# The order of the small loads on GpSimd's DMA queue at the start of a linear-attention and mixture-of-experts layer

## The reference

```
xn   = layernorm(x)
q,k,v= split(xn @ w_qkv.T + b_qkv)           # 16 heads of 64
q    = silu(q);  k = softmax(k over tokens)
kv   = k^T v per head;  o = q @ kv per head
o    = layernorm(o) * ln_g + ln_b
gate = sigmoid((xn @ w_g1.T + b_g1) @ w_g2.T + b_g2)
attn = (o * gate) @ w_out.T + b_out
logits = xn @ Wr.T; the two best of 8 experts, softmax over the two
ffn  = sum over the two of w * (xn @ We[e]), tokens past a capacity of 769 dropped
out  = x + attn + ffn
```

## Time and profile before

| | us |
|---|---|
| median of 3 runs | 1163.08 (1161.27 to 1163.39) |
| the profiled execution's own time | 1163.06 |
| its span, slowest core (core 0) | 1161.3 |
| spans of the 8 cores | 1150.5 to 1161.3 |
| TensorE busy | 873.4 (75%) |
| DVE busy | 452.8 (39%) |
| ACT busy | 103.6 (9%) |
| POOL busy | 57.8 (5%) |

### The profile page before, as it was taken

The page is one execution under the profiler, slowest core; times in us unless marked ns, Lnnn a source line. Parts: engine busy times, 40 slices in busy tenths (PEclk is TensorE's granted clock), DMA queues, the critical chain, the costliest instruction groups (busy, mean ns, idle before and its releaser), DMA issues.

```text
span 1161.3 us, 11087 instructions; the slowest of 8 cores (1150.5 to 1161.3 us)
## 1 busy us (share of the span) xinstructions
PE 873.4 (75%) x3848; PEld 356.4 (31%) x3914; DVE 452.8 (39%) x692; ACT 103.6 (9%) x123; POOL 57.8 (5%) x58
## 2 busy tenths in 40 slices
PE   0133063499997999650555999999999999999993
PEld 0010021133335433110101334444444444444441
DVE  0123867400332001737685334444444444444441
ACT  0121100122000221141221000000000000000000
POOL 2100000000000000000000000000000000000244
PEclk9975577699998899575555999999999999999997
DMA  2466600000404002200000004040404132231276
GB/s 48 109 169 151 114 1 18 19 1 1 73 1 73 1 1 34 39 0 0 1 1 0 1 1 73 1 73 1 73 6 68 22 53 36 38 50 24 66 242 236
DMA packets 23300, 55.59 MB, mean 48 GB/s; under 512 B 4752, under 2 KB 4752, under 8 KB 22224
## 3 DMA queue, kind: packets, MB, share of 16 engines
q0 software_dynamic: 16160, 29.68, 16.6%
q1 hardware_dynamic: 4208, 12.63, 3.8%
q10 hardware_dynamic: 2880, 12.58, 2.9%
HBM read 76.18 MB, written 8.39 MB: 73 GB/s over the span
## 4 chain that ended last, share of the span: by engine, by line
PE 62%; DVE 17%; DMA 13%; issue 4%; ACT 2%; DVEq 1%; POOL 0%; POOLq 0%; ACTq 0%
PE PS L167 62%; DMA ar<-x_fm 6%; DMA y<-fpool 5%; DVE scr_b L177 5%; DVE ar L177 5%; DVE srow L177 3%; DVE reps L177 1%; ACT bpool L184 1%; DVE qrow L177 1%; DMA wg_sb<-wg_t 1%; ACT qrow L184 1%; DVEq L176 1%; DVE drow L177 0%; DVE crow L177 0%; DMA wr_hi<-wr_t 0%
## 5 line engine op out<-in xcount | busy, mean ns | idle before, releaser
L167 PE MATMUL PS<-ar 128*128 128x512 bf16 (+1 forms) x3135 | 698.2, 377 | 21.2 <-DVE ar L177 9.8
L167 PEld LDWEIGHTS PS<-ar 128*128 128x128 bf16 x3200 | 301.9, 99 | 382.6 <-issue 52.9
L177 DVE SCALAR_TENSOR_TENSOR ar<-PS,lc,ar 128x512 bf16<-128x512 f32 x256 | 192.2, 751 | 251.1 <-PE PS L167 251.1
L177 DVE CAST ar<-PS 128x512 bf16<-128x512 f32 x96 | 66.4, 692 | 167.7 <-PE PS L167 164.5
L167 PE MATMUL PS<-ar,ones_c_b 128*1 128x512 bf16 x64 | 22.5, 487 | 93.4 <-ACT bpool L184 93.1
L177 DVE TENSOR_TENSOR ar<-fpool,ar 128x2048 bf16<-128x2048 f32 x8 | 18.3, 2293 | 90.7 <-DMA ar<-x_fm 90.7
L184 ACT ACTIVATE ar<-PS 128x512 bf16<-128x512 f32 x64 | 38.2, 597 | 93.8 <-PE PS L167 93.7
L198 POOL DMA_DIRECT2D ar<-we x8 | 7.0, 873 | 665.8 <-PE PS L167 665.8
L167 PE MATMUL PS<-bpool,wg_sb 64*128 64x512 bf16 x32 | 18.7, 584 | 28.4 <-DVE ar L177 28.4
L167 PEld LDWEIGHTS PS<-ar,ones_c_b 128*1 128x1 bf16 x64 | 5.2, 92 | 109.2 <-issue 106.8
L191 POOL TENSOR_TENSOR fpool<-ar,fpool 128x1024 f32<-128x1024 bf16 x16 | 34.2, 2137 | 89.9 <-DVE ar L177 62.3
(11 more groups left out here) (109 smaller groups left out, 267.2 us busy)
## 6 DMA issues: line engine op xcount, KB each, us to landing
ar<-we POOLq DMA_DIRECT2D x8, 2048.0 KB, 16.9
fpool<-x_tm SPq DMA_DIRECT2D x16, 512.0 KB, 4.2
y<-fpool ACTq DMA_DIRECT2D x16, 512.0 KB, 4.1
fpool<-x_fm SPq DMA_DIRECT2D x4, 1024.0 KB, 10.0
ar<-x_fm POOLq DMA_DIRECT2D x8, 512.0 KB, 7.2
fpool<-x_fm ACTq DMA_DIRECT2D x4, 1024.0 KB, 7.0
ar<-wk_t POOLq DMA_DIRECT2D x1, 2048.0 KB, 16.7
ar<-wv_t POOLq DMA_DIRECT2D x1, 2048.0 KB, 14.9
```

The lines of the kernel that those rows point to most:

```text
L167: i = eng.matmul(out, l, r, start=start, stop=stop)
L177: getattr(eng, name)(*a, **k).then_inc(S["dv"], 1)
```

## The change

The block of eleven small transfers on "d2" is taken from ahead of the x stage. Nine of them (`wr_hi` first, then `ltri`, `ident` and the six biases) are issued behind the x stage, ahead of `wk`; `wg1` and `wg2` are issued behind `wv`. TensorE gets two waits on "d2": ahead of the transposes of the logits (for `ident` and `ltri`) and ahead of the gate's hidden layer (for `wg1` and `wg2`). `t_bias` is set and used nowhere.

```diff
--- before.py
+++ after.py
@@ -207,18 +207,6 @@
                 gps("memset", ones_c_b[:], 1.0, inc=False)
                 gps("memset", ones_c_f[:], 1.0, inc=False)
                 t_const_gp = gps("memset", eps_sb[:], EPS)
-                dma("d2", ltri_sb[:], ltri)
-                dma("d2", ident_bf[:], ident[0:8, 0:8])
-                dma("d2", wg1_sb[:], wg1_t.rearrange("(c p) o -> p c o", p=128))
-                dma("d2", wg2_sb[:], wg2_t)
-                dma("d2", bq_sb, bq)
-                dma("d2", bk_sb, bk)
-                dma("d2", bv_sb, bv)
-                dma("d2", bg1_sb, bg1)
-                dma("d2", bg2_sb, bg2)
-                dma("d2", bo_sb, bo)
-                t_wrhi = dma("d2", wr_hi[:], wr_t.rearrange("(c p) e -> p c e", p=128))
-
                 t_xbf = []
                 t_stats_h = []
                 t_sq_h = []
@@ -257,8 +245,19 @@
                     t_stats_h.append(c["pe"])
                 t_stats_pe = c["pe"]
                 t_xlo = c["dv"]
+                t_wrhi = dma("d2", wr_hi[:], wr_t.rearrange("(c p) e -> p c e", p=128))
+                dma("d2", ltri_sb[:], ltri)
+                t_ltri = dma("d2", ident_bf[:], ident[0:8, 0:8])
+                dma("d2", bq_sb, bq)
+                dma("d2", bk_sb, bk)
+                dma("d2", bv_sb, bv)
+                dma("d2", bg1_sb, bg1)
+                dma("d2", bg2_sb, bg2)
+                t_bias = dma("d2", bo_sb, bo)
                 t_wk = dma("d2", wkv[:, 0, :, :], wk_t.rearrange("(c p) o -> p c o", p=128))
                 t_wv = dma("d2", wkv[:, 1, :, :], wv_t.rearrange("(c p) o -> p c o", p=128))
+                dma("d2", wg1_sb[:], wg1_t.rearrange("(c p) o -> p c o", p=128))
+                t_wg = dma("d2", wg2_sb[:], wg2_t)
                 w("vector", "gp", t_const_gp)
                 w("vector", "pe", t_stats_pe)
                 for tb in range(TB):
@@ -361,6 +360,7 @@
                 t_lgt_hl = dve("tensor_tensor", lgt_lo[:, :], lgt_f[:, :], lgt_hi[:, :],
                                ALU.subtract)
                 w("tensor", "dv", t_lgt_hl)
+                w("tensor", "d2", t_ltri)
                 for tc in range(NT):
                     mm(bank(4)[:, 8 * tc:8 * (tc + 1)],
                        lgt_hi[:, 128 * tc:128 * (tc + 1)], ident_bf[0:8, 0:8],
@@ -571,6 +571,7 @@
                     bnk = 4 + tb % 2
                     if tb == 0:
                         w("tensor", "dv", t_kv3)
+                        w("tensor", "d2", t_wg)
                     if tb >= 2:
                         w("tensor", "dv", g_ev[tb - 2])
                     for h in range(HC):
```

## The result

The changed kernel takes 1132.46 us in the median of 8 runs (1131.02 to 1135.49), against 1162.97 for the kernel before (8 runs, 1161.27 to 1163.47): a ratio of 0.9744, interval 0.9732 to 0.9756, 30.5 us less. The forecast was 1130.6, in a range of 1127 to 1138.

A forecast was written before the change was run, and what follows sets the result against it. POOL's serial transfers, eleven small ones then eight bf16 x loads, were taken to bound the start. -34.3 + 1.8 + 0 + 0 = -32.5 us from 1163.1 gave 1130.6 us, range 1127 to 1138.

The forecast's parts named there:

- Removed ahead of x: Head of POOL's queue: without the eleven transfers the first x load starts at 3.12 instead of 37.46, 34.34 us earlier.
- What the stage gives back: x stage: 0.6 of float32 piece 0 spills into the third beat (one bf16 load to the next), costing 1.8 us.
- Behind x: POOL's queue after the x loads: the moved transfers land before anyone needs them and cost 0 on the path.
- the copy that had been named: DVE's copy ahead of the offsets, at 182.3, waiting for POOL's second memset: called the tightest place.
- Rival C: POOL's offsets memset comes so late that DVE's copy waits past its old date: slower, 1175.6 us at 2.2 times; 3%.
- slack of 38 us: POOL's chain behind x could run 38 us later in all before DVE's copy ahead of the offsets waits.
- The waits added on TensorE: The two added TensorE waits on "d2" cost nothing, as both values are reached long before.
- The clock: TensorE's clock falls to half behind the x stage; last sum matmuls or K projection may shift 1.7 us either way; taken 0.
- Rival A: x stage: the early collision never clears, every beat carries three loads, giving back 29.1 us: 1157.9; 6%, mostly in partial form.
- Rival B: POOL's transfers are held from 99.7 until DVE ends the normalisation at 161.0; DVE waits 23.5 us: 1154.1; 2%.
- noise on another core: Core 0 is slowest, core 7 1.1 us behind; another core becoming slowest adds only a little, 2 us in the range.

The follow-up runs named there:

- the control: The changed kernel once more, unaltered, on the chip of some of the follow-up kernels: 1130.05 us, ratio 0.9727 to the kernel before.
- 12 more: The changed kernel with the last bias load (`bo`) repeated 12 more times on POOL's queue behind x: 1132.35 us, ratio 0.9743 to the kernel before.
- 36 more: The changed kernel with the last bias load (`bo`) repeated 36 more times on POOL's queue behind x: 1171.36 us, ratio 1.0081 to the kernel before.
- the experiment with SP's constants: The changed kernel with SP's router weights, gam and bet issued behind the x stage, float32 piece 0 ahead: 1132.61 us, ratio 0.9750 to the kernel before.

## Why the prediction was right, and where it was off

*Removed ahead of x, 34.3.* Right in kind, 0.9 too large. The first load starts at 3.12 on every core; 34.34 was core 0's figure, the mean over the cores is 33.4. The forecast speaks of 2 to 6 us "for a few KB"; wg1 and wg2 are 128 KB each. That it is the serial wait that costs is shown by the kernel without those waits.

*What the stage gives back, 1.8.* The size is near, and the working is not, so that it is near is luck. Four profiles have the changed stage up to the end of x (the change, the control, 12 more, 36 more): 69.7, 68.1, 68.5 and 68.3 us in the mean of the cores, against 67.6 before, so 0.5 to 2.1 more, 1.0 in their mean. I had float32 piece 0 issued at 7.75 and 0.6 of it left over. It was issued at 11 to 15, with all of it left, and it did not cost 3.06 either. The third beat, 6.19 in the mean before, was 6.27 after; it is the first two that grew, from 6.0 and 11.5 to 7.0 and 12.3. What the experiment with SP's constants shows in its place: in the first beats an earlier load slows its neighbour, so the price of a load can't be placed in one beat.

*Behind x, 0.* Right, and tested from both sides: 12 more transfers changed nothing, 36 more cost 39.0 us (1171.36 against 1132.35 for 12 more, on the same chip), and DVE's wait at the copy that had been named is 39.5. Rival C is a true mechanism, with the wrong size for this change. The forecast's slack of 38 us was a little short of the 44 to 47 that the runs show. The estimate of where the mechanism decides was also near: it was to make a slower kernel only past a chain of 139 us, and the longer chain was 146 (from 73.7 to the memset at 219.5) and slower by 9.4 us.

*The waits added on TensorE, 0.* Right: from the reciprocal to the copy of the totals, with the first of the two waits in between, the time is the same within 0.1 us, and the second lies in the part that comes next.

*The clock, 0 with 1.7 either way.* No change that can be told: four matmuls of the last group of sums took 1.86 us before and 1.86 on core 4 after, and the part behind the sums' copy is 1048.4 and 1047.9 us in the mean.

*Rival A* (three loads in every beat) did not occur: long and short beats still alternate. *Rival B* (POOL can't issue beside DVE) did not occur as a held queue, but see the last section.

*The rest, 1.9 us* (1132.46 against 1130.6; by the control's ratio it is 0.6). The forecast moved core 0 of one execution as if it stood for all, and said that noise on another core can add only a little. Here is the step that was mis-sized. 0.9 us of it can be core 0's late start, as said above. The step also left out that the slowest core is a different one from execution to execution and lies some way off the mean: by 3.5 us in the profile before, by 2.3 to 7.4 (4.2 in the mean) in 26 other executions of the kernel before (beside the experiments), and by 3.0 to 6.6 (4.7 in the mean) in 9 executions of the changed kernel. So the 28.6 us between the slowest cores of the two profiles compare a near one (3.5) with the farthest of the nine (6.6), and are not a loss by the change: on the control's chip the distance is 4.7 before and 3.9 after, and the mean over the cores fell by 31.1 us, from 1155.3 (10 executions) to 1124.3 (4). Of the 1.4 us between this and the forecast's 32.5, 0.9 can be core 0's start again; the rest is open.

Where the distance comes from can be seen in part in the stage of each core:

| x stage, us, cores 0/1, 2/3, 4/5, 6/7 | | | | |
|---|---|---|---|---|
| before | 69.7 / 67.0 | 68.1 / 66.3 | 67.4 / 65.6 | 66.5 / 70.4 |
| after | 66.2 / 70.5 | 66.8 / 71.0 | 73.7 / 70.0 | 67.8 / 72.0 |
| control | 65.4 / 69.2 | 71.0 / 67.5 | 70.0 / 65.7 | 70.0 / 66.2 |
| 12 more transfers | 71.2 / 67.0 | 70.5 / 66.5 | 70.3 / 66.1 | 70.0 / 66.2 |

In each pair of neighbours one core is ahead, by some 4 us in the three later rows and by 2 to 4 before; which of the two it is changes from run to run. In the three later rows the one that is behind is also the one whose float32 piece 0 was issued at 13.8 us or later, the other at 11 to 12.5. The late issue is a sign of the handicap and not its cause: the pattern stays in the kernel that loads next to nothing of piece 0, and also in the one that issues piece 0 at 1.13 on every core, where the two of a pair lie 3.3 to 9.0 us apart. So neighbours share something on the way from memory; that is inferred from the pairs and was not tested by itself. Before, the cores began their x loads between 34.6 and 38.5 us, now all at 3.12. In the whole span this makes the loser of a pair lose no more than it did: the two of a pair lie 4.4 us apart in the 26 executions before and 4.5 in the nine after. On the slowest core of each of the four profiles the stage is 73.7, 71.0, 71.2 and 70.6 us, against 69.7 on core 0 before: 1.9 more in the mean.

## What to carry to other kernels

A queue that waits for each landing turns small transfers into a delay for each, here 2.2 to 5.7 us for 0.1 to 128 KB. Look at the head of each queue for what nobody needs yet and put it behind the first large load, or drop the waits between them; then list what stands behind the moved ones on the same engine, and find the first instruction that would wait: that gives the slack, and here it was right within 10 us. When the large loads come to the front they are the next bound: count their bytes (here x was read twice), their buffers and the engine behind them before tuning the order of the rest, since in a stage as full as this one an earlier load only slowed its neighbour.

## What the runs showed of the hardware

A small transfer takes long beside a large one. From gam's issue to the next it was 1.9 to 2.2 us before, and 4.8 to 6.4 beside a 1 MB read; POOL waited 5.92 us for bq (2 KB) in place of 1.76.

GpSimd and VectorE do lock each other out, which the rows before the change had not shown. POOL's issues of small transfers take 0.49 us, but on each of the eight cores one took 0.88 to 1.52, not the same one on all. On core 4, POOL and then DVE:

```profile
87.27 0.49 POOL L198 DMA_DIRECT2D bias_b<-bk  x1 [1.86 <-DMA bias_a<-bq]
89.64 1.47 POOL L198 DMA_DIRECT2D bias_b<-bv  x1 [1.88 <-DMA bias_b<-bk]
```

```profile
89.79 1.21 DVE L177 TENSOR_SCALAR drow<-qrow 1x2048 bf16<-1x2048 f32 x1
```

The issue ends at 91.11, 0.11 us behind the end of DVE's operation at 91.00. On all eight cores the long issue is the one that lies beside this kind of DVE operation (TENSOR_SCALAR), and it ends 0.09 to 0.11 us behind it. That is the rule of the Trainium skill (SBUF: State Buffer, on its two separate sides): of a VectorE operation in a two-port mode and GpSimd's, the one that comes second is blocked till the other ends. The trace agrees, though it does not show the mode, nor which of the two asked first: the issue's row begins 0.15 us ahead of DVE's. It also shows which operations do not hold POOL here: beside DVE's subtraction of two tensors the issue took 0.53, and on core 4 beside a copy out of PS 0.49. In the kernel with 12 more transfers it also went the other way, on cores 0 and 1. On core 0, POOL, then DVE:

```profile
164.01 0.97 POOL L191 MEMSET scr_b<- 128x1024 bf16 x1
165.10 1.00 POOL L191 MEMSET srow<- 1x8 f32 x1
```

```profile
163.83 2.23 DVE L177 CAST bpool<-fpool 8x2048 bf16<-8x2048 f32 x1
```

The same cast takes 1.22 us in the profile of the change, where no memset lies beside it. Here it and the memset of 8 numbers (0.10 us elsewhere) each took 1 us longer. Both cases cost about 1 us, and only the cast stood on the path.
